# Attention softmax by single heads instead of pairs of heads, weight transposes alternating one by one, and the next panel's input transposes placed inside the output projection

## The reference

```python
x = src                                            # (8, 2048, 1024) f32
n1 = layernorm(x)
q, k, v = n1 @ Wq + bq, n1 @ Wk + bk, n1 @ Wv + bv # 8 heads of 128, blocks of 64 tokens
scores = einsum('bnqhd,bnkhd->bhnqk', q, k) * 128 ** -0.5
out = einsum('bhnqk,bnkhd->bnqhd', softmax(scores), v)
x = x + out @ Wo + bo
h = square(relu(layernorm(x) @ W_fc.T))            # 4096 wide
y = h @ W_proj.T
mem = 0                                            # 5 steps of
mem = 0.9 * mem + y - (mem > 1); spk = (mem > 1)   # a membrane with reset
x = x + sum(spk) / 5
```

## Time and profile before

| | |
|---|---|
| time, median of 3 runs (lowest to highest) | 1217.94 us (1215.89 to 1218.53) |
| time of the profiled execution | 1217.53 us |
| its span on the slowest core, core 4 | 1215.7 us |
| spans of the other cores | 1198.2 to 1212.9 us |
| PE, DVE, ACT, POOL busy, share of the span | 68%, 39%, 33%, 21% |
| softmax stages of panels 0, 1, 2, 3 on core 4 | 98.2 to 178.8, 245.1 to 321.3, 386.2 to 461.9, 528.3 to 584.5 us |
| first feed-forward matmul | 615.8 us |

### The profile page before, as it was taken

One profiled execution on the slowest core, in us unless ns is written; L12 is line 12 of the kernel. 1 busy time (PEld: TensorE's weight loads), 2 busy tenths in 40 slices (PEclk: granted clock), 3 DMA queues, 4 the chain that ended last, 5 costly groups with the idle time before them and its releaser, 6 DMA issues.

```text
span 1215.7 us, 18923 instructions; the slowest of 8 cores (1198.2 to 1215.7 us)
## 1 busy us (share of the span) xinstructions
PE 825.9 (68%) x6600; PEld 601.0 (49%) x6624; DVE 478.9 (39%) x481; ACT 406.2 (33%) x841; POOL 254.0 (21%) x122
## 2 busy tenths in 40 slices
PE   0394139933597327963789797978979797988910
PEld 0143123422243213432368686867768686877810
DVE  0105112142203403052310664829375573928276
ACT  3131232213131232311144444454444444444410
POOL 3000010001000100000000443507153351616254
PEclk9996559966699558985889898999999899998965
DMA  9993561034600453006658695959779595959700
GB/s 169 210 217 52 114 111 28 1 61 91 126 1 1 88 120 70 1 14 134 199 160 275 206 311 174 316 175 314 238 248 323 174 316 191 324 194 313 259 35 35
DMA packets 127290, 194.18 MB, mean 160 GB/s; under 512 B 42208, under 2 KB 44256, under 8 KB 127200
## 3 DMA queue, kind: packets, MB, share of 16 engines
q1 hardware_dynamic: 108144, 151.03, 40.9%
q0 software_dynamic: 14448, 33.56, 15.1%
q10 hardware_dynamic: 4608, 8.39, 1.8%
HBM read 192.95 MB, written 25.17 MB: 179 GB/s over the span
## 4 chain that ended last, share of the span: by engine, by line
PE 56%; DMA 19%; ACT 8%; DVE 8%; issue 5%; SPq 1%; POOL 1%; ACTq 0%; DVEq 0%; POOLq 0%
PE psC L831 16%; DMA w2scratch<-w2stage 10%; PE psA L865 8%; PE psB L865 8%; DMA w1slab<-w1scratch 5%; DMA bv_sb<-bv 3%; PE psA L636 3%; PE psA L328 3%; PE psB L636 2%; PE psA L367 2%; PE psB L348 2%; PE psB L367 2%; PE psB L328 2%; PE psA L348 2%; PE psD L550 2%
## 5 line engine op out<-in xcount | busy, mean ns | idle before, releaser
L831 PE MATMUL psC<-xn2t_sb,w1slab 128*128 128x256 bf16 x2048 | 275.3, 280 | 18.7 <-ACT xn2t_sb L769 11.8
L831 PEld LDWEIGHTS psC<-xn2t_sb,w1slab 128*128 128x128 bf16 x2048 | 204.4, 100 | 50.2 <-issue 22.4
L842 ACT ACTIVATE h_bf<-psC 128x256 bf16<-128x256 f32 x256 | 97.6, 381 | 224.5 <-PE psC L831 224.3
L865 PE MATMUL psA<-h_bf,w2slab 128*128 128x256 bf16 x1024 | 154.3, 273 | 24.6 <-ACT h_bf L845 23.7
L932 POOL TENSOR_TENSOR acc_q<-acc_q,spk_q 128x2048 bf16<-128x2048 bf16 (+1 forms) x27 | 148.3, 5494 | 73.1 <-DVE spk_q L928 73.1
L865 PE MATMUL psB<-h_bf,w2slab 128*128 128x256 bf16 x1024 | 153.9, 273 | 0.0
L936 DVE SCALAR_TENSOR_TENSOR mem_q<-mem_q,y_sb 128x2048 f32<-128x2048 f32 (+1 forms) x27 | 142.8, 5289 | 2.8
L865 PEld LDWEIGHTS psA<-h_bf,w2slab 128*128 128x128 bf16 x1024 | 98.3, 98 | 44.5 <-issue 33.2
L845 ACT ACTIVATE h_bf<-h_bf 128x256 bf16<-128x256 bf16 x256 | 106.7, 417 | 23.5
L196 POOL DMA_DIRECT2D wtmp<-Wpr x16 | 8.6, 539 | 484.3 <-PE psD L550 484.3
L865 PEld LDWEIGHTS psB<-h_bf,w2slab 128*128 128x128 bf16 x1024 | 100.4, 98 | 11.8
(11 more groups left out here) (98 smaller groups left out, 997.0 us busy)
## 6 DMA issues: line engine op xcount, KB each, us to landing
w2slab<-w2scratch SPq DMA_DIRECT2D x128, 512.0 KB, 6.5
w1slab<-w1scratch SPq DMA_DIRECT2D x128, 512.0 KB, 7.6
x_sb<-x SPq DMA_DIRECT2D x4, 2048.0 KB, 44.0
wtmp<-Wpr POOLq DMA_DIRECT2D x16, 512.0 KB, 7.2
wtmp<-Wfc POOLq DMA_DIRECT2D x32, 256.0 KB, 8.4
w2scratch<-w2stage SPq DMA_DIRECT2D x32, 256.0 KB, 3.4
w1scratch<-w2stage ACTq DMA_DIRECT2D x32, 256.0 KB, 4.5
out<-x_sb POOLq DMA_DIRECT2D x16, 512.0 KB, 8.4
```

Source lines behind the costliest of these rows:

```text
L831: op("pe", lambda E, fc=fc, c=c, hp=hp, s1b=s1b: E.matmul(hp, s1b[:, c * 128:(c + 1) * 128], xn2t_sb[:, c * 256:(c + 1) * 256], start=(c = ...
L842: op("se", lambda E, fc=fc, hp=hp: E.activation(h_bf[fc % 2][:], hp, ACT.Relu), inc="se")
L865: E.matmul(tgt[:, mc * 256:(mc + 1) * 256], slb[:, m * 128:(m + 1) * 128], h_bf[fp % 2][:], start=(fp == 0 and m % 2 == 0), stop=(fp == 31 ...
```

## The change

Three things are changed; the data computed, the loads and the stores stay the same.

1. **Heads one by one.** The softmax tiles are halved (256 columns) and there are two of each, `p_bf` and `pt_bf` included. `scores`, `softmax_pre`, `exp_h`, `softmax_post`, `pt_h` and `ptev_h` work on one head; a buffer is reused two heads later. `pt_h` uses the half `h % 2` of `psD` alone.
2. **Weight groups alternate.** Each head now handles one w2 group and one w1 group, so `gidx` is even for all w2 groups and odd for all w1 groups. A w2 copy on DVE waits for the previous w2 store, a w1 copy on ACT for the previous w1 store.
3. **Input transposes of the next panel.** The four groups of step 1 become `xn1t_group(p, jj)`. For panels 1 to 3 each is called behind the output projection of tile jj of the panel before, ahead of the DVE addition. The norm parts are spread by heads: part 1 at heads 1 to 4, part 2 at head 5, part 3 at head 6, where it now stands before the last head's work.

```diff
-        scores(0)
-        E_sb = scores(1)
-        softmax_pre(0, E_sb)
-        exp_u(0)
-        scores(2)
-        E_sb = scores(3)
-        softmax_pre(1, E_sb)
-        exp_u(1)
-        softmax_post(0)
-        pt_u(0)
-        ptev_u(0)
-        for u in range(4):
...
+        E_s0 = scores(0)
+        softmax_pre(0, E_s0)
+        exp_h(0)
+        E_s1 = scores(1)
+        softmax_pre(1, E_s1)
+        exp_h(1)
         softmax_post(0)
-        pt_u(0)
-        ptev_u(0)
+        pt_h(0)
+        ptev_h(0)
+        for h in range(8):
+            if h + 2 < 8:
+                E_s = scores(h + 2)
+                softmax_pre(h + 2, E_s)
+                exp_h(h + 2)
+            if h + 1 < 8:
+                softmax_post(h + 1)
+                pt_h(h + 1)
+                ptev_h(h + 1)
+            pv_h(h)
+            attnev_h(h)
+            ci = 4 * p + h // 2
+            if h % 2 == 0:
+                wait("pe", *E_ld2[ci])
+            w2_group(ci, h % 2)
+            fcw = 8 * p + h
+            wait("pe", *E_w1ld[fcw])
+            w1_group(fcw)
             if p + 1 < PA:
+                if 1 <= h <= 4:
+                    ln1_part1(p + 1, h - 1)
+                elif h == 5:
                     ln1_part2(p + 1)
+                elif h == 6:
                     ln1_part3(p + 1)
...
-            wait("ve", "pe", n["pe"])
+            E_opj = n["pe"]
+            if p + 1 < PA:
+                xn1t_group(p + 1, jj)
+            wait("ve", "pe", E_opj)
```

More of the change, by code:

```diff
@@ L60, in build_nc @@
     attn_sb = regC.enter_context(nc.sbuf_tensor("attn_sb", [128, 4096], BF16))
[L61 to L65, removed]
+    s_f32 = [e(nc.sbuf_tensor(f"s_f32_{i}", [128, 256], F32, side="right"))
+             for i in range(2)]
+    p_bf = [e(nc.sbuf_tensor(f"p_bf_{i}", [128, 256], BF16, side="right"))
+            for i in range(2)]
+    pt_bf = [e(nc.sbuf_tensor(f"pt_bf_{i}", [128, 256], BF16, side="right"))
+             for i in range(2)]
     ident = e(nc.sbuf_tensor("ident", [128, 128], BF16, side="right"))
@@ L290, in build_nc, with xn1t_group @@
     ln1_part3(0)
+    E_xn1t_d = {}
+    def xn1t_group(p, jj):
+        if jj == 0:
+            wait("pe", "ve", E_xn1_d[p])
+            if p == 0:
+                wait("pe", "gp", E_ident)
+        pe_wait_rel(relD[jj % 2])
+        for c in range(8):
+            op("pe", lambda E, jj=jj, c=c: E.transpose(
+                psD[:, (jj % 2) * 1024 + c * 128:
+                    (jj % 2) * 1024 + (c + 1) * 128],
+                xn1_bf[:, jj * 1024 + c * 128:jj * 1024 + (c + 1) * 128],
+                ident[:]), inc="pe" if c == 7 else None)
+        fill = n["pe"]
+        wait("se", "pe", fill)
+        dst = bass.AP(xn1t_sb[:].tensor, jj * 128,
+                      [[4096, 128], [512, 8], [1, 128]])
+        src = psD[:, (jj % 2) * 1024:(jj % 2) * 1024 + 1024].rearrange(
+            "p (c t) -> p c t", c=8)
+        op("se", lambda E, dst=dst, src=src: E.copy(dst, src),
+           inc="se")
+        relD[jj % 2] = ("se", n["se"])
+        E_xn1t_d[(p, jj)] = n["se"]
+        if jj == 3:
+            E_xn1t_fill_prev[0] = fill
     for p in range(PA):
-        wait("pe", "ve", E_xn1_d[p])
         if p == 0:
[L295 to L315, removed]
+            for jj in range(4):
+                xn1t_group(0, jj)
         E_qe, E_ke = [0] * 8, [0] * 8
-        wait("pe", "se", E_xn1t[3])
+        wait("pe", "se", E_xn1t_d[(p, 3)])
         if p == 0:
@@ L436, in softmax_post, with exp_h @@
-        def softmax_post(u):
-            wait("ve", "se", E_exph[u])
-            wait("ve", "ve", war["p"])
[L439 to L442, removed]
+        def exp_h(h):
+            wait("se", "ve", E_tta[h])
+            op("se", lambda E, h=h: E.activation(
+                s_f32[h % 2][:], s_f32[h % 2][:], ACT.Exp), inc="se")
+            E_exph[h] = n["se"]
@@ L451, in softmax_post @@
                 ALU.mult), inc="ve")
-            E_p[u] = n["ve"]
+            E_p[h] = n["ve"]
             war["p"] = n["ve"]
[L455 to L478, removed]
+        def pt_h(h):
+            wait("pe", "ve", E_p[h])
+            pe_wait_rel(relD[h % 2])
+            base = (h % 2) * 1024
+            for t_ in range(2):
+                op("pe", lambda E, h=h, t_=t_, base=base: E.transpose(
+                    psD[:, base + t_ * 128:base + (t_ + 1) * 128],
+                    p_bf[h % 2][:, t_ * 128:(t_ + 1) * 128], ident[:]),
+                    inc="pe" if t_ == 1 else None)
+            E_pt[h] = n["pe"]
@@ L480, in pv_h, with ptev_h @@
+        def ptev_h(h):
+            wait("se", "pe", E_pt[h])
+            base = (h % 2) * 1024
+            op("se", lambda E, h=h, base=base: E.copy(
+                pt_bf[h % 2][:], psD[:, base:base + 256]), inc="se")
+            E_ptev[h] = n["se"]
+            relD[h % 2] = ("se", n["se"])
         def pv_h(h):
-            u = h // 2
-            wait("pe", "se", E_ptev[u])
+            wait("pe", "se", E_ptev[h])
             if h < 2:
@@ L494, in pv_h @@
                 col = (bl % 2) * 512 + (bl // 2) * 64
[L495 to L496 removed]
+                op("pe", lambda E, h=h, bl=bl, tt=tt, kb=kb, qc=qc, col=col,
+                   pair=pair: E.matmul(
                        pair[:, col:col + 64],
```

106 lines of the change are left out of this document (35 added, 71 removed).

## The result

The changed kernel takes 1156.33 us (median of 10 runs, lowest 1154.15) against 1217.71 for the kernel before (10 runs): a ratio of 0.950, 95% interval 0.948 to 0.952. The forecast was 1155.

The account below looks back on a forecast made before the run. It took the softmax stages to be bound by a chain of waits through one slow w2 store per unit. Stages 59.6 plus transposes 3.8 save 63.4 us from 1217.5: 1154.1, forecast 1155 us, range 1128 to 1200.

Parts of the forecast that it names:

- What bounds the kernel: Softmax stages: no engine full, a chain of waits; a w2 store of 10.87 to 10.98 us fills over half a unit.
- Prices of half-size operations: Softmax on 256 columns: a DVE operation takes 0.45 us, an exponential on ACT about 0.42, a copy on ACT 0.36.
- Prologue: Stage start, from the first score to the first weight transpose finished: 9.8 us.
- Odd to even, 7.9 us: Period from an odd head's w2 copy on DVE to the next head's: 7.9 us, 2.15 over the engine chain.
- I take a w1 store of 6.7: Odd head's w1 store, issued right behind its w2 store, lands in 6.7 us, between its median and its maximum.
- rival B: Odd heads' w2 stores stay as slow as now, landing after 10.9 us; 19.3 us saved, 1198 us in all; chance 0.16.
- Even to odd, 6.95 us: Engine chain from an even head's w2 copy on DVE to the next, with `ln1_part1` on ACT: 6.95 us.
- End of the stage: Last heads: 6.9 us at head 5, inside the 7.9 taken; then 4.6 us from head 6's copy to the output projection.
- Third part, 3.8 us: Input transposes moved inside the output projection: PE's 5.02 us per panel becomes 3.75, three times 1.25 saved, 3.8 us.
- The total: Whole kernel: 63.4 us saved from the profiled 1217.5 us, giving a forecast of 1155 us.

Follow-up runs that it names:

- experiment 4: Norm part 3 moved behind head 7 in the changed kernel: 1164.19 us, 0.954 of the kernel before; with four staging tiles as well, 1126.25 us, 0.917.

## Why the prediction was right, and where its steps were off

**What bounds the kernel: right.** The stage was a chain through one slow store per unit, and the gain came from letting engine work run beside it. The runs with one part each show it: with the store in front of ACT's copies the stages of panels 0 to 2 are 75 to 84 us on the slowest core whatever the size of the heads, with the alternation 62 to 66 even in pairs.

**Prices of half-size operations: right.** DVE 0.42 for 0.45 worked out, exponential 0.42 for 0.42, probability copy 0.37 for 0.36. The result of a head on DVE (L506) stayed at 0.75 us, since it was already one instruction per head before; I had halved it to 0.47 by mistake, which is off the chain except at head 7.

**Prologue: right.** The first w2 transposes end 9.1 us into the stage in panel 1, against 9.8.

**Odd to even, 7.9 us: wrong.** It is 11.5, 9.7 and 10.7 in panel 1. This is the step "I take a w1 store of 6.7". The w2 store sets it, with a landing of 8.8 to 10.6, and that is close to rival B's value (10.9) rather than mine. I argued that most of the store would be through before the load's data began; the traces with the load moved or left out show that the load beside it does decide, and with the load issued 0.4 us ahead the store gets no head start. Nor is it late "however early it was issued", as the prediction put it under rival B: 1.0 us ahead of the load is enough. The w1 store is close behind as a limit: at head 4 ACT's copy, which waits for it, starts at 263.69 and DVE's at 264.46, which is why a quick w2 store alone saved so little.

**Even to odd, 6.95 us: wrong the other way.** It is 5.1 us. I had put PE's w1 transposes, ACT's weight copy and its norm part 1 on the chain there, all behind DVE's copy. But PE and ACT don't stand while DVE does: the next scores end at 245.7, 3.9 us before DVE's copy at 249.61, and ACT's weight copy starts at 248.50, so that the norm (250.0 to 252.4) lies beside DVE's softmax. With four staging tiles, where DVE hardly waits, the same periods are 7.1 and 6.6 us, as worked out. In panel 1 the three odd periods cost 8.2 us more than forecast, the two even ones 3.7 less, the prologue, the first period and the end 1.2 less: 61.6 for 58.2, after rounding. The stages came to 237.5 for 229.2, 8 us more. Rival B was nearly right on the landing, but its panel 1 of 69.9 us is 8.3 too long, since it kept the even periods at 6.95 and took the full 10.9 three times.

**End of the stage: half right.** 4.4 us for 4.6 (the terms given add up to 4.5), with the cost of the norm as said; the head's result took 0.28 more than I had put, and closer spacing of the operations gave it back. But that the norm would be better elsewhere doesn't follow, see experiment 4.

**Third part, 3.8 us: low.** Undone it costs about 7 us. The order on PE gives about what was worked out: the three passages are 3.2 us shorter on the slowest cores than before. The clock at the start of Q, which the earlier trace rows showed (15 matmuls in 5.02 us) and the sum left out, gives another 2.7.

**The total** of 1155 is better than its terms, and that is luck. The spans of the slowest cores, 1215.7 and 1155.7 us, differ by 60.0 where the sum had 63.4. The stages gave 51.1 (59.6 in the sum) and the passages 3.2 (3.8); what the sum didn't count gave 5.7: the clock at Q in panels 1 to 3 2.7, the entry into panel 0 1.6 (core 0 at 96.7 us, core 4 before at 98.2, with the same code up to there), and small differences behind the last stage 1.5. Within the stages two errors of opposite sign, in the odd and the even periods, partly cancelled as well.

## What to carry to other kernels

Look at what stands behind a wait on its engine before making the awaited thing quicker: here three lines of order gave 3.6%, two more staging tiles another 2.4%, and a quicker w2 store no gain in time clear of noise, because the next store ended just as late. While one engine stands in a wait the others run ahead, so the period behind a long wait is shorter than a chain counted from an even start; the work that has moved into the wait must not be added again. Halving operations has its price on every hop between engines: without the new order it cost 0.9%, with it it gained 0.8%, and with four staging tiles the stages were shorter without it.

## What the runs showed of the hardware that was not expected

A w2 store of 256 KB in 256-byte pieces landed in 2.5 to 3.1 us at even heads of panel 1, with no `Wpr` load issued just before it, and in 8.8 to 10.6 us at odd heads beside a 512 KB load issued 0.4 us ahead of it. With that load issued 1.0 us behind the store it landed in 2.7 to 3.6 us, and in the one case where the load came 0.1 us behind it in 9.9. With the transposes in a block behind the projection PE began Q at either 1.2 or 2.4 GHz after the same order of instructions, on different cores and panels of one run (41.3 against 43.0 us for the same work); with 2 us instead of 5 between the projection and Q it began at 2.4 GHz in panels 1 to 3 on every core traced.
